# Storing a kernel's text keys from GpSimd's DMA queue instead of ScalarE's, in a fused cross-attention kernel on one Trainium2 core

## What is computed

```python
N_TXT, N_OBJ, N_OTH, N_IP = (77, 4, 4, 16)
ehs_txt = encoder_hidden_states[:, :77]
ehs_obj = encoder_hidden_states[:, 77:81]
ehs_oth = encoder_hidden_states[:, 81:85]
ehs_ip  = encoder_hidden_states[:, 85:]          # 427 rows
q = _heads(hidden_states @ to_q_w)
h_txt = _sdpa(q, _heads(ehs_txt @ to_k_w), _heads(ehs_txt @ to_v_w))
...
out = _merge(h_txt) + _merge(h_obj) + _merge(h_oth) + _merge(h_ip)
out = out @ to_out_w + to_out_b + residual
```

## Time and profile before

| | us |
|---|---|
| median of 3 runs | 2464.65 (2462.13 to 2473.61) |
| the profiled execution's own time | 2463.14 |
| its span in the trace | 2461.5 |
| TensorE busy | 2400.6 (98%) |
| VectorE busy | 1862.4 (76%) |
| ScalarE busy | 1778.2 (72%) |
| GpSimd busy | 412.1 (17%) |
| 16 DMA engines, queue of SyncE (q1) | 293232 packets, 55.6% |
| 16 DMA engines, queue of ScalarE (q10) | 53398 packets, 7.6% |

### The profile page before, as it was taken

One profiled execution on the slowest core, in us unless ns is written; L12 is line 12 of the kernel. 1 busy time (PEld: TensorE's weight loads), 2 busy tenths in 40 slices (PEclk: granted clock), 3 DMA queues, 4 the chain that ended last, 5 costly groups with the idle time before them and its releaser, 6 DMA issues.

```text
span 2461.5 us, 37404 instructions
## 1 busy us (share of the span) xinstructions
PE 2400.6 (98%) x12801; PEld 1815.4 (74%) x12801; DVE 1862.4 (76%) x3288; ACT 1778.2 (72%) x3909; POOL 412.1 (17%) x567
## 2 busy tenths in 40 slices
PE   7999999999999999999999999999999999999998
PEld 7999999999999984566666666666666666666654
DVE  3357777732333478999999999999999999999982
ACT  3343433322222369999999999999999999999994
POOL 0000000000000023412222223123122122122210
PEclk9999999999999999999999999999999999999999
DMA  9645444374554657667766667676767677676761
GB/s 279 161 143 160 151 138 141 108 260 168 210 180 164 200 130 151 128 125 154 152 128 141 145 140 151 124 145 149 138 148 141 126 156 150 126 146 140 144 125 50
DMA packets 346821, 370.10 MB, mean 150 GB/s; under 512 B 94335, under 2 KB 241919, under 8 KB 346631
## 3 DMA queue, kind: packets, MB, share of 16 engines
q1 hardware_dynamic: 293232, 304.79, 55.6%
q10 hardware_dynamic: 53398, 62.93, 7.6%
HBM read 215.57 MB, written 83.89 MB: 122 GB/s over the span
## 4 chain that ended last, share of the span: by engine, by line
PE 88%; DVE 7%; ACT 2%; DMA 1%; issue 1%; ACTq 1%; SPq 0%
PE st_ps L1498 16%; PE s_ps L439 12%; PE om_ps L491 11%; PE st_ps L459 11%; PE om_ps L473 11%; PE om_ps L514 8%; PE s_ps L1550 7%; PE om_ps L1550 4%; PE s_ps L1518 3%; PE st_ps L1550 3%; DVE negmax L667 3%; ACT s_ps L607 1%; ACT probs L599 1%; DVE neglse L702 1%; DMA qpack<-q_out 1%
## 5 line engine op out<-in xcount | busy, mean ns | idle before, releaser
L607 ACT ACTIVATE s_ps<-s_ps,negmax 128x427 f32<-128x427 f32 x1280 | 767.7, 608 | 24.8 <-DVE small L676 24.7
L667 DVE TENSOR_REDUCE negmax<-s_ps 128x2 f32<-128x854 f32 x640 | 665.4, 1040 | 91.2 <-PE s_ps L439 84.7
L599 ACT ACTIVATE probs<-st_ps 128x1024 f32<-128x1024 f32 x632 | 656.0, 1038 | 53.8 <-PE st_ps L459 37.6
L1498 PE MATMUL st_ps<-ctx_split,w_split 128*128 128x428 f32 (+2 forms) x2280 | 431.7, 350 | 10.5 <-DVE k_out L1378 10.1
L439 PE MATMUL s_ps<-kpack,qpack 96*128 96x512 f32 x1280 | 427.2, 415 | 8.9 <-ACT s_ps L607 5.8
L1498 PEld LDWEIGHTS st_ps<-ctx_split,w_split 128*128 128x128 f32 x2280 | 412.5, 190 | 28.5 <-DVE k_out L1378 11.3
L459 PE MATMUL st_ps<-qpack,kpack 104*128 104x512 f32 x1264 | 411.4, 407 | 9.3 <-ACT probs L599 8.6
L400 POOL TENSOR_TENSOR small<-small,negmax 128x616 f32<-128x616 f32 x160 | 196.5, 1228 | 1113.8 <-DVE negmax L684 1113.8
L491 PE MATMUL om_ps<-xs,wq 128*128 128x512 f32 x1200 | 348.7, 401 | 21.6 <-DVE out L747 21.6
L439 PEld LDWEIGHTS s_ps<-kpack,qpack 96*128 96x128 f32 x1280 | 224.5, 191 | 193.6 <-ACT s_ps L607 89.3
L514 PE MATMUL om_ps<-heads,wo 128*128 128x512 f32 x1125 | 322.8, 394 | 0.0
(11 more groups left out here) (103 smaller groups left out, 2332.9 us busy)
## 6 DMA issues: line engine op xcount, KB each, us to landing
kpack<-kT SPq DMA_DIRECT2D x240, 256.0 KB, 4.2
qpack<-q_out SPq DMA_DIRECT2D x240, 256.0 KB, 7.6
kT<-k_out ACTq DMA_DIRECT2D x160, 217.5 KB, 3.3
ctx_split_raw<-in_ctxT SPq DMA_DIRECT2D x128, 214.0 KB, 4.7
tok_pair<-in_ctxT SPq DMA_DIRECT2D x48, 512.0 KB, 4.5
xs_raw<-in_xT SPq DMA_DIRECT2D x85, 256.0 KB, 4.6
out<-in_xT SPq DMA_DIRECT2D x75, 256.0 KB, 5.6
out_yT<-out SPq DMA_DIRECT2D x75, 256.0 KB, 2.1
```

What stands on the lines that cost most here:

```text
L599: nc.scalar.activation(probs[:, at:at + 2, :], transposed(u, duo), ACT.Exp).then_inc(p_done, 1)
L607: last = nc.scalar.activation(s_ps[:, n % 2, z, SMALL:TOK], s_ps[:, n % 2, z, SMALL:TOK], ACT.Exp, bias=negmax[:, r, IP, j, t:t + 1], accu ...
L667: nc.vector.tensor_reduce(negmax[:, r, IP, j, t0:t0 + 2], s_ps[:, n % 2, :, SMALL:TOK], AX_X, ALU.max, negate=True).then_inc(s_max, 1)
L1498: last = nc.tensor.matmul(k_place(run, m)[:, 0:n], w[name][:, pw, q, m * P:(m + 1) * P], c[b][:, px, q, a:a + n], start=(q == 0 and z == 0 ...
```

## The change

The 40 text-key stores are issued by GpSimd, each pair after a wait for the block's low part, in the order of the blocks and before GpSimd's first other work. They count on five semaphores of their own, `kt_stored`; ScalarE's evictions of text blocks and of the first image block wait on these, and SyncE waits on them before the quarters. The counts on `k_stored` now begin with the image runs. ScalarE issues no text-key store.

```diff
@@ project_context
     k_stored = [sem(f"k_stored{r}") for r in range(KR)]
+    kt_stored = [sem(f"kt_stored{r}") for r in range(KR)]
@@ sync_part
         sp.wait_ge(t_done, 1)
         for r in range(KR):
-            sp.wait_ge(k_stored[r], 32 * TXT)
+            sp.wait_ge(kt_stored[r], 32 * TXT)
...
         for r in range(KR):
-            sp.wait_ge(k_stored[r], 32 * (TXT + 1))
+            sp.wait_ge(k_stored[r], 32)
...
         for r in range(KR):
-            sp.wait_ge(k_stored[r], 32 * RUNS)
+            sp.wait_ge(k_stored[r], 32 * BATCH)
@@ scalar_part, keep_k
             if k0 >= KR:
-                act.wait_ge(k_stored[k0 % KR], 32 * (k0 // KR))
+                if run <= TXT:
+                    act.wait_ge(kt_stored[k0 % KR], 32 * (k0 // KR))
+                else:
+                    act.wait_ge(k_stored[k0 % KR], 32 * (k0 // KR - TXT))
@@ scalar_part, store_k
             act.wait_ge(k_lo, k0 + 1)
-            if not is_txt(run):
-                act.wait_ge(k_fill, k0 - k_base(TXT) + 1)
+            act.wait_ge(k_fill, k0 - k_base(TXT) + 1)
             for part in (HI, LO):
-                if not is_txt(run):
-                    dst = d["kT"][run - TXT, part, rows, N_TXT:TOK]
-                    src = k_out[:, k0 % KR, part, 0:SM + IPN - 1]
-                else:
-                    dst = d["kT"][slice(*TXT_BATCHES[run]), part, rows, 0:N_TXT].rearrange("b p t -> p b t")
-                    src = k_out[:, k0 % KR, part, 0:k_cols(run)[2]].rearrange("p (b t) -> p b t", t=N_TXT)
-                nc.scalar.dma_start(dst, src.bitcast(F32)).then_inc(k_stored[k0 % KR], 16)
+                nc.scalar.dma_start(d["kT"][run - TXT, part, rows, N_TXT:TOK],
+                                    k_out[:, k0 % KR, part, 0:SM + IPN - 1].bitcast(F32)).then_inc(k_stored[k0 % KR], 16)
@@ scalar_part, store
-            if kind == "k":
+            if kind == "k" and not is_txt(a):
                 store_k(a, b)
@@ gpsimd_part
+        def store_text(run, m):
+            k0, rows = k_base(run) + m, slice(m * P, (m + 1) * P)
+            pool.wait_ge(k_lo, k0 + 1)
+            for part in (HI, LO):
+                nc.gpsimd.dma_start(d["kT"][slice(*TXT_BATCHES[run]), part, rows, 0:N_TXT].rearrange("b p t -> p b t"),
+                                    k_out[:, k0 % KR, part, 0:k_cols(run)[2]].rearrange("p (b t) -> p b t", t=N_TXT)
+                                    .bitcast(F32)).then_inc(kt_stored[k0 % KR], 16)
+
+        for run in range(TXT):
+            for m in range(QC):
+                store_text(run, m)
         pool.wait_ge(ks_lo, 2)
```

## The result

The kernel after takes 2472.36 us (median of 22 runs, 2468.41 to 2479.08), the kernel before 2464.49 us (22 runs). The ratio is 1.003, with a 95% interval of 1.0023 to 1.0038: slower by 0.3%, where 0.45% faster was forecast (2453.5 against 2464.65). The time lies in the stated range and in "within 0.5%", but it moved the other way.

A forecast was written before the change was run, and what follows sets the result against it. ScalarE's blocked text-key store issues were taken to bound the text stage. The 14.1 us ceiling shrank to 11.5 through store landings, less 1 gave 10.5: 2463.1 to 2452.6, median forecast 2453.5 us; range 2448 to 2500.

The forecast's parts named there:

- within 0.5%: Outcome for the whole kernel's time: a change of no more than 0.5% either way, given a chance of 0.45.
- What bounds the stage: Text-key stage: ScalarE's store issues, blocked by full DMA engines, were 25.3% of the chain and delayed TensorE.
- The ceiling of 87.5 us: Text-key stage: at full TensorE pace it ends at 87.5 us instead of about 101.6, winning 14.1 us.
- Removed from ScalarE: Text-key stage: 40 DMA issues and 20 waits leave ScalarE, so eviction and splits follow inputs at once; alone the ceiling.
- p: Cost of one GpSimd DMA issue, taken as about 0.5 to 1 us and bounded above by 5.76 us.
- The first rival: Text stores: GpSimd's issues become the bound; gain gone at 2.46 us an issue, +37 us at 3.6; chance 0.40.
- One of its signs: End of the text stage: SyncE's quarters of v_ip later than 110 us would show the forecast wrong.
- Loads: ... now near 53 us ... Covered: SyncE issues the last text group's context near 53 us, landing in 9.0 us median, before its need at 76.4 us.
- The rate of the stores: Text-key stores pass 235 packets a us beside the loads and 370 after them; a wide pair takes 5.4 or 3.5 us.
- The second rival: Text-key stage: stores fall behind SyncE's loads, gain near zero, 2458 to 2470 us; chance 0.06.
- The rule that speaks against the change: DMA issue: all issuers share the same 16 engines, so spreading saves only issue time; here that sits on the chain.
- The end of the stage: Text stores to v_ip quarters: the last store may land 3.6 us later; TensorE needs the values 19.9 us after.

The follow-up runs named there:

- e7: Kernel before, stores still on ScalarE, with the last text group's context loaded ahead of the v_txt weights; ratio 0.9987, 2457.41 us.
- e12: Kernel before, with the last text group's context loaded after the first half of the second small weights and v_txt weights last; ratio 0.9968, 2455.07 us.
- e1: Kernel after, each text store writing only its group's first batch, other rows filled later by copies, output different; ratio 1.0045, 2471.11 us.
- e6: Kernel after, with the last text group's context loaded after the first half of the second small weights and v_txt weights last; ratio 0.9989, 2456.59 us.
- run 2: Not an experiment: the kernel's third group of text-key blocks, the first narrow one; to the second small product 14.7 us before, 33.5 after.
- e3: Kernel after, GpSimd waiting for a block's two stores to land before issuing the next block's, two in flight; ratio 1.0128, 2491.88 us.
- e9: Kernel after, with single_packet=True asked for on the text stores; the trace shows no change of framing; ratio 1.0025, 2468.45 us.
- e4: Kernel after, with only the wide text stores issued from GpSimd and the narrow ones from ScalarE; ratio 1.0019, 2465.85 us.
- e11: Kernel after, at most four GpSimd stores in flight and the last text group's context loaded ahead of the v_txt weights; ratio 0.9965, 2453.50 us.
- e10: Kernel after, with at most four GpSimd stores in flight and the load order unchanged; ratio 0.9988, 2458.48 us.
- e5: Kernel after, unchanged and measured again beside other runs; ratio 1.0029, 2466.42 us.

## Why the prediction was wrong

- **What bounds the stage, right.** ScalarE's blocked issues held the chain, and the cause was busy DMA engines: with other loads beside the same stores they blocked less (e7, e12). The ceiling of 87.5 us was met by e1 at 87.10.
- **"Removed from ScalarE", right in kind, the times in part by luck.** Run 1 ended at 54.64 us where 52.5 was worked out. Its evictions waited for landings as foreseen: they began at 35.98, 43.27, 45.56 and 51.14 us against landings forecast for 36.3, 41.7, 47.1 and 52.5. But the forecast let the pairs land one behind the other, each 2.1 us after its packets at 235 packets a us. In the trace the queue was faster and up to ten stores shared it, so that a wide store took 13.3 us from issue to landing (median). Two errors went against each other.
- **p, right.** 0.83 us median where 0.5 to 1 was taken. The first rival (0.40) falls with it: break-even was 2.46 us. One of its signs came all the same, the quarters later than 110 us (115.39), so that sign could not tell the rival from what happened. The first-byte figure of about 1 us in the Trainium skill, DMA: Bandwidth & Descriptors, section Specifications, was taken for the price of an issue; the issue's own row has 0.76 to 1.04, and no row here shows the first byte.
- **"Loads: ... now near 53 us ... Covered" is the step that failed**, first by when SyncE is free to issue that load. Its other two numbers would not have held either.
  - *When the context is issued.* It took SyncE to be ready when run 1 ended. In the trace before it had been idle since 51 us, and I kept that for the kernel after without asking what the unblocked stores do to SyncE's issues. They came at 74.53 us and not near 53.
  - *How long it takes to land.* 9.0 us was a number of the kernel before. In the kernel after it took 8.0 us (median), but from 74.53 us on, when run 1's stores were all issued. In e6 SyncE was ready as the prediction had it, at 52.05 us, and the context took 16.7 us to land and still cost TensorE 6.57 us.
  - *When it is needed.* Not at run 3's start, 76.4 us. ScalarE splits it during run 2, ahead of block (2,1)'s eviction, which the prediction's own timetable has at 64.9 us. The cover was about 12 us and not 23. In the trace ScalarE began to wait for it at 62.4 us.

  The DMA engines were full before the change, so whatever the stores got sooner the loads had to get later; I had written the full shares down and priced only one side. That the wait reached TensorE through the place of the splits in ScalarE's program is read from the timeline; no run moved the splits.
- **The rate of the stores.** 235 packets a us beside the loads was taken from a queue throttled by its blocked issuer. After, 1.02 MB in the 8 us from 38 are 3310 pieces of 308 bytes, 414 a us; in the next two stretches of 8 us it was 337 and 345 (0.83 and 0.85 MB). The second rival had the right resource and the wrong loser: it let the stores fall behind the loads.
- **The rule that speaks against the change.** The Trainium skill, DMA: Bandwidth & Descriptors, section Issuing engines are not separate DMA queues, says that all issuers share the same engines and that spreading saves only issue time. It was set aside because issue time was on the chain. The trace agrees that the engines are shared: the stores' share rose from 36.4 to 72.8% and the loads' fell from 78.6 to 33.2%. What the runs add is that the issue time saved on ScalarE was spent on SyncE.
- **The end of the stage, right.** From transposes to quarters 4.9 us (110.51 to 115.39), 5.4 before; e3 hit its 19.9 us within 0.6.

What stays open: whether GpSimd's queue would take more of the engines than a hardware queue with as many stores in flight. Its packets are about 3 KB (1.02 MB in 329), SyncE's about 1 KB; e9 was to vary this and did not. e4's possible 0.1% is not explained either, nor e1's wait of 17.0 us.

## What to carry to other kernels

A DMA issue that blocks its engine is also a throttle. Here, taken off the critical engine without another limit on how much is in flight, it let the backlog move to the next issuer, the queue of loads. Of the three limits that were run the middle one was best: two in flight lost 1.28%, four won 0.12%, up to ten lost 0.3%. Where the DMA engines are full, ask first which bytes could go later: the order of the loads alone gave as much as the best kernel with the change (e12 and e11). And ask of each load not when its data is multiplied but when any engine's program first waits for it.

## What was not expected of the hardware

- The share of a queue went with the stores in flight: 18.8% with two, 24.5% with four, 72.8% with up to ten (38 to 46 us, e3, e10, after), while SyncE's went from 87.6 over 80.5 to 33.2%. What both moved together fell too: 2.69, 2.36 and 1.45 MB.
- The time of a GpSimd issue grows far less than its pieces: in e1 0.54 us median for 128; in after 0.76 for the 384 of the narrow and 0.87 for the 640 of the wide stores (1.52 and 1.74 a pair).
- Two profiled executions of one program (after and e5) differ by 5.6 us in the stage where the queues compete, and by 5.3 us in the span.
